# Cross-attention scores from high and low parts made ahead, and another order of the small steps around them

## The reference

```python
def _L0_xattn_ref(hidden_q, kv_c, ...):          # hidden_q = layernorm(x): 64 x 32 x 512, kv_c: 64 x 257 x 128
    q_hk = (hidden_q @ Wq.T).reshape(Bv, Sv, H, K)                 # 16 heads
    q_big = _apply_rope(jnp.einsum('bshk,hkq->bshq', q_hk, w_kc_q), sin_q, cos_q)
    kv_r = _apply_rope(kv_c, sin_k, cos_k)
    q_r = jnp.einsum('bshq,hqr->bhsr', q_big, W_qr)
    k_r = jnp.einsum('bld,hdr->bhlr', kv_r, W_kr)
    scores = jnp.einsum('bhsr,bhlr->bhsl', q_r, k_r)
    attn = jax.nn.softmax(scores, axis=-1)
    ctx_c = jnp.einsum('bhsl,bld->bhsd', attn, kv_r)
    ctx_lat = jnp.einsum('bhsd,hkd->bhsk', ctx_c, w_kc_kv)
    return ctx_lat.transpose(0, 2, 1, 3).reshape(Bv, Sv, H * K) @ Wo.T
```

## Time and profile before

| | us |
|---|---|
| median of 3 runs | 1603.32 (1601.59 to 1603.51) |
| the profiled execution | 1603.56 |
| its span, first to last instruction | 1601.4 |
| its mean granted TensorE clock | 0.972 of full speed |
| TensorE busy over the span | 1485.5 (93%) |
| VectorE busy | 1139.9 (71%) |
| ScalarE busy | 811.1 (51%) |
| GpSimd busy | 541.8 (34%) |

### The profile page before, as it was taken

One profiled execution on the slowest core, in us unless ns is written; L12 is line 12 of the kernel. 1 busy time (PEld: TensorE's weight loads), 2 busy tenths in 40 slices (PEclk: granted clock), 3 DMA queues, 4 the chain that ended last, 5 costly groups with the idle time before them and its releaser, 6 DMA issues. The chain is left out here.

```text
span 1601.4 us, 26509 instructions
## 1 busy us (share of the span) xinstructions
PE 1485.5 (93%) x8136; PEld 1123.1 (70%) x8136; DVE 1139.9 (71%) x1820; ACT 811.1 (51%) x1739; POOL 541.8 (34%) x594
## 2 busy tenths in 40 slices
PE   4799999999978999999999977999898899999997
PEld 3577777777746777777777766888443478787876
DVE  6888777887648788788788853777687735556466
ACT  4566565666545555555555543555211355554554
POOL 4244333442025554544545513221351202222021
PEclk9899999999989999999999988999898899999999
DMA  4223334243565444544544514000244100000000
GB/s 152 68 81 111 105 110 119 75 122 95 182 219 126 119 119 105 125 111 106 129 107 108 139 21 172 0 0 0 84 174 158 45 1 1 27 1 26 0 27 27
DMA packets 140917, 140.05 MB, mean 87 GB/s; under 512 B 84150, under 2 KB 111926, under 8 KB 139708
## 3 DMA queue, kind: packets, MB, share of 16 engines
q1 hardware_dynamic: 140284, 138.54, 30.0%
q10 hardware_dynamic: 576, 0.81, 0.2%
HBM read 109.88 MB, written 27.39 MB: 86 GB/s over the span
## 5 line engine op out<-in xcount | busy, mean ns | idle before, releaser
L997 ACT ACTIVATE c_e<-c_sc_ps,c_peak 128x257 f32<-128x257 f32 x256 | 119.6, 473 | 219.4 <-DVE c_peak L900 219.4
L878 POOL TENSOR_TENSOR c_mixed_low<-c_whole,c_mixed_high 128x512 fp32r<-128x512 f32 x64 | 81.9, 1279 | 211.0 <-ACT c_mixed_high L1017 211.0
L77 DVE TENSOR_TENSOR b_rot_parts_low<-b_rot,b_rot_parts_high 128x1536 fp32r<-128x1536 f32 x64 | 136.0, 2125 | 21.9 <-ACT b_rot_parts_high L541 21.9
L278 POOL TENSOR_TENSOR b_turned_raw<-b_turn_part 128x384 f32<-128x384 f32 x32 | 70.1, 2190 | 166.2 <-DVE b_key_parts_low L77 165.0
L1571 PE MATMUL f_ps<-f_right,f_left 128*128 128x512 f32 x256 | 115.7, 613 | 8.4 <-ACT f_raw L1614 6.1
L70 PE MATMUL c_out_ps<-c_shared_high,c_mixed_high 128*128 128x512 f32 x256 | 112.2, 438 | 11.1 <-issue 10.1
L324 DVE TENSOR_TENSOR b_rot<-b_w_qr,b_angle 128x1536 f32<-128x1536 f32 x64 | 119.2, 1862 | 0.2
L70 PE MATMUL b_ps<-c_shared_high,b_wq_parts_high 128*128 128x512 f32 x256 | 108.5, 424 | 6.5 <-DVE c_shared_low L77 6.5
L70 PE MATMUL e_mm_ps<-folded_high,e_h_t_high 128*128 128x512 f32 x256 | 106.4, 416 | 5.7 <-DVE e_h_t_low L77 5.6
L541 ACT ACTIVATE b_rot_parts_high<-b_rot 128x1536 fp32r<-128x1536 f32 x64 | 95.3, 1489 | 24.5 <-PE b_ps L72 17.0
L274 POOL TENSOR_TENSOR b_turn_part<-b_early,b_centre 128x384 f32<-128x384 f32 x64 | 82.1, 1303 | 72.2 <-DMA b_early<-early 70.5
(11 more groups left out here) (232 smaller groups left out, 3903.8 us busy)
## 6 DMA issues: line engine op xcount, KB each, us to landing
c_ends_spread<-end_weights SPq DMA_DIRECT2D x64, 256.0 KB, 4.3
carried_queries<-x SPq DMA_DIRECT2D x7, 2048.0 KB, 11.3
b_early<-early SPq DMA_DIRECT2D x15, 640.0 KB, 4.0
f_left<-ent_in SPq DMA_DIRECT2D x16, 512.0 KB, 5.4
f_right<-ent_out SPq DMA_DIRECT2D x16, 512.0 KB, 6.5
c_q_first<-carried_queries SPq DMA_DIRECT2D x32, 224.0 KB, 3.3
c_q<-carried_queries SPq DMA_DIRECT2D x32, 224.0 KB, 3.2
b_late<-late SPq DMA_DIRECT2D x16, 320.0 KB, 3.8
```

What stands on the lines that cost most here:

```text
L77: return nc.vector.tensor_tensor(low, value, high.bitcast(F32), ALU.subtract)
L878: nc.gpsimd.tensor_tensor(mixed[1][:, w, :, u], whole[:, u % 2].rearrange("p (h s) -> p h s", h=H), mixed[0][:, w, :, u].bitcast(F32), ALU ...
L997: last = nc.scalar.activation(e[:, v, c], sc_ps[:, 2 * v + c, 0:L], ACT.Exp, bias=peak[:, v, c:c + 1], accum_out=total[:, v, c:c + 1])
```

## The change

1. Scores: each 128x257 fp32 product becomes three fp32r products (`multiply_parts`) of high and low parts of the queries and of the keys, with the keys padded to 258 columns (a zero column). ScalarE makes the high parts (`round_queries`, `round_keys`) and GpSimd the low parts (`split_queries`, `split_keys`), two batches ahead.
2. `keep_ends` goes from GpSimd to VectorE, after `find_peak`.
3. The keys' turn goes from half 0 to half 1, its rounding too, and `split_kv` to the next batch's even step, after `find_peak`.
4. SyncE: the store of the ends is taken out of `spread_ends` and goes ahead of the batch's raw loads; the raw keys have two buffers instead of four; a batch's queries are loaded after the spread; before `holo.load` SyncE waits for the last rotation, because `part` now lies in `spare`.
5. The last two heads of the first two batches' queries are no longer copied by ScalarE but loaded from `staged` (`staged_queries`), after the last output weights.
6. The angles of the next part are made in three pieces instead of two; `keep_moments` goes to j = 6 and `square_row` to j = 4.

Cut to its core:

```diff
             crossing.output_weights(sp, w_vo_dram, 2)
+            sp.wait_ge(qc_stored, 8 * HPAIRS)
+            crossing.staged_queries(sp, staged)
...
-                    if isinstance(U, int) and U >= 2 * HPAIRS - 2:
-                        at = (H - 2 + ab) * S + base
-                        nc.scalar.activation(crossing.q[:, :, at:at + G], ps[:, QC_BANK + ab].rearrange("p (b s) -> p b s", b=B)[:, 0:2], ACT.Copy)
...
+    def staged_queries(self, sp, staged):
+        for u in range(2):
+            sp.dma_start(self.q[:, u, (H - 2) * S:].bitcast(F32), staged[:, u].rearrange("p h s -> p (h s)")).then_inc(self.q_loaded[u], 16)
...
-        part = sb("c_part", [P, 2, L])
+        part = spare[:, 0:2 * L].rearrange("p (n l) -> p n l", n=2)
+        q_high = sb("c_q_high", [P, 2, H * S], F32R)
+        keys = pair("c_key", [P, 2, LE])
...
+            def store_ends(i, u):
+                b, v = BT * i + u, u % 2
+                sp.wait_ge(ended, 2 * b + 2)
+                sp.dma_start(ends_dram[bass.ds(b, 1)].rearrange("b p c -> p (b c)"), ends[:, v]).then_inc(ends_stored[v], 16)
+
             def spread_ends(i, u):
...
-                wait(sp, mix_taken, b - 1)
-                sp.wait_ge(ended, 2 * b + 2)
-                sp.dma_start(ends_dram[at].rearrange("b p c -> p (b c)"), ends[:, v]).then_inc(ends_stored[v], 16)
                 sp.wait_ge(ends_stored[v], 32 * i + 16 * (u // 2) + 16)
...
-                    if known(i, 1):
-                        wait(sp, rotated_, b - BT + 1)
-                        crossing.load(sp, b, u)
                     if isinstance(b, int) and b < 2:
                         continue
-                    wait(sp, scored, 2 * (b - BT) + 2)
-                    sp.dma_start(q[u][:, 0:(H - 2) * S], ...
-                    sp.dma_start(q[u][:, (H - 2) * S:], ...
+                    if known(i, 1):
+                        store_ends(i - 1, u)
+                    wait(sp, rotated_, b - 1)
+                    crossing.load(sp, b, u % 2)
                     if known(i, 1):
                         spread_ends(i - 1, u)
+                    wait(sp, scored, 2 * (b - BT) + 2)
+                    sp.dma_start(q[u][:, 0:(H - 2) * S].bitcast(F32), ...
+                    sp.dma_start(q[u][:, (H - 2) * S:].bitcast(F32), ...
...
             in_tiles(sp, tile)
+            sp.wait_ge(rotated_, B)
             holo.load(sp, holo_loaded)
             for u in range(BT):
+                store_ends(TILES - 1, u)
                 spread_ends(TILES - 1, u)
...
             def rotate(b, u, tile_of_b):
-                pool.wait_ge(raw_loaded[u], 48 * (tile_of_b + 1))
+                pool.wait_ge(raw_loaded[u % 2], 48 * (2 * tile_of_b + u // 2 + 1))
...
-            def keep_ends(n, i, u, half):
-                pool.wait_ge(normed, n + 1)
...
+            def split_queries(b, u):
+                pool.wait_ge(q_rounded, b + 1)
+                nc.gpsimd.tensor_tensor(q[u], q[u].bitcast(F32), q_high[:, u % 2].bitcast(F32), ALU.subtract).then_inc(q_split, 1)
+
+            def split_keys(b, u):
+                pool.wait_ge(key_rounded, b + 1)
+                nc.gpsimd.tensor_tensor(keys[1][:, u % 2], kv_even[u], keys[0][:, u % 2].bitcast(F32), ALU.subtract).then_inc(key_split, 1)
...
-                    keep_ends(n, i, u, half)
+                    if half == 0 and not (isinstance(b, int) and (b == 0 or b + 1 >= B)):
+                        split_keys(b + 1, (u + 1) % BT)
                     if half == 0 and not (isinstance(b, int) and b + 2 >= B):
                         rotate(b + 2, (u + 2) % BT, i + (u + 2) // BT)
+                    if half == 1 and not (isinstance(b, int) and b + 2 >= B):
+                        split_queries(b + 2, (u + 2) % BT)
                     if half == 1 and (u or known(i, 1)):
                         split_mixed(b - 1, (u - 1) % BT, w if u else 1 - w)
...
+            def keep_ends(n, i, u, half):
+                v = u % 2
+                if half == 0:
+                    wait(dve, ends_stored[v], 32 * i + 16 * (u // 2))
+                nc.vector.tensor_tensor(ends[:, v, 2 * half:2 * half + 2], e[:, half, :, END], inverse[:, half], ALU.mult).then_inc(ended, 1)
...
                         find_peak(n + 1, 1 - half)
+                    keep_ends(n, i, u, half)
+                    if half == 0 and (u or known(i, 1)):
+                        split_kv(b - 1, (u - 1) % BT)
                     if half == 1 and (u or known(i, 1)):
                         add_end(i - (u == 0), (u - 1) % BT)
                     if more:
                         normalise(n + 1, 1 - half)
                     split_turned(n, u, half)
-                    if half == 0:
-                        split_kv(b, u)
...
-            dve.wait_ge(scored, 2 * B)
+            dve.wait_ge(rotated_, B)
...
+            def round_queries(b, u, t):
+                act.wait_ge(q_loaded[u], queries_in(u, t))
+                wait(act, scored, 2 * b - 2)
+                nc.scalar.activation(q_high[:, u % 2], q[u].bitcast(F32), ACT.Copy).then_inc(q_rounded, 1)
+
+            def round_keys(b, u):
+                act.wait_ge(rotated_, b + 1)
+                wait(act, scored, 2 * b - 2)
+                nc.scalar.activation(keys[0][:, u % 2], kv_even[u], ACT.Copy).then_inc(key_rounded, 1)
...
                     round_turned(n, b, u, half)
-                    if half == 0:
+                    if half == 1:
                         round_kv(b, u)
                     if half == 1 and (u or known(i, 1)):
                         round_mixed(b - 1, (u - 1) % BT, i if u else i - 1, w if u else 1 - w)
+                    if not (isinstance(b, int) and b + 2 >= B):
+                        if half == 0:
+                            round_queries(b + 2, (u + 2) % BT, i + (u + 2) // BT)
+                        else:
+                            round_keys(b + 2, (u + 2) % BT)
...
+            round_keys(0, 0)
+            round_queries(0, 0, 0)
             exponential(0, 0)
+            round_keys(1, 1)
+            round_queries(1, 1, 0)
...
                 if half == 0:
-                    pe.wait_ge(q_loaded[u], queries_in(u, t))
-                    pe.wait_ge(rotated_, b + 1)
+                    pe.wait_ge(q_split, b + 1)
+                    pe.wait_ge(key_split, b + 1)
...
-                    last = nc.tensor.matmul(sc_ps[:, 2 * half + c, 0:L], q[u][:, at], kv_t[u], start=True, stop=True)
+                    last = multiply_parts(nc, sc_ps[:, 2 * half + c, 0:LE], [q_high[:, u % 2, at], q[u][:, at]], [a[:, u % 2] for a in keys], True, True)
...
-                    if half == 0:
+                    if half == 1:
                         turn_kv(b, u)
```

More of the change, by code:

```diff
@@ L691, in __init__ @@
         raw, swapped = sb("c_raw", [P, 2, L]), sb("c_swapped", [P, 2, L])
+        self.raw_pair, self.swapped_pair = raw[:], swapped[:]
         self.raw, self.swapped = ([a[:, u] for u in range(2)] for a in (raw, swapped))
-        self.q = sb("c_q_first", [P, 2, H * S])
-        self.keys = sb("c_keys_first", [P, L])
+        self.q = ctx.enter_context(nc.sbuf_tensor("c_q_first", [P, 2, H * S], F32R))
+        self.keys = sb("c_keys_first", [P, L + 1])
         self.q_loaded = [sem(f"c_q_loaded{u}") for u in range(BT)]
-        self.pool_chained, self.rotated = sem("c_pool_chained"), sem("c_rotated")
+        self.pool_chained, self.rotated, self.padded = sem("c_pool_chained"), sem("c_rotated"), sem("c_padded")
         self.table_loaded = sem("c_table_loaded")
-        self.raw_loaded = [sem(f"c_raw_loaded{u}") for u in range(BT)]
+        self.raw_loaded = [sem(f"c_raw_loaded{u}") for u in range(2)]
         self.staged_out = sem("b_staged_out")
@@ L730, in rotate_first @@
         nc.gpsimd.tensor_tensor(part[:, 1], self.swapped[0], self.table[:, 1], ALU.mult).then_inc(self.pool_chained, 1)
+        nc.gpsimd.memset(self.keys[:, L:], 0.0).then_inc(self.padded, 1)
         pool.wait_ge(self.pool_chained, 2)
-        nc.gpsimd.tensor_tensor(self.keys[:], part[:, 0], part[:, 1], ALU.add).then_inc(self.rotated, 1)
+        pool.wait_ge(self.padded, 1)
+        nc.gpsimd.tensor_tensor(self.keys[:, 0:L], part[:, 0], part[:, 1], ALU.add).then_inc(self.rotated, 1)
     def first(self, sp):
@@ L844, in tile @@
                              x_tiles[bass.ds(i, 1)].rearrange("t p d -> p (t d)")).then_inc(x_loaded, 16)
-            for u in range(2, BT):
-                crossing.load(sp, u, u)
             in_tiles(sp, tile)
+            sp.wait_ge(rotated_, B)
             holo.load(sp, holo_loaded)
             for u in range(BT):
+                store_ends(TILES - 1, u)
                 spread_ends(TILES - 1, u)
@@ L858, in rotate @@
             def rotate(b, u, tile_of_b):
-                pool.wait_ge(raw_loaded[u], 48 * (tile_of_b + 1))
-                nc.gpsimd.tensor_tensor(part[:, 0], raw[u], table[:, 0], ALU.mult).then_inc(pool_chained, 1)
```

(17 more changed lines are left out.)

43 lines of the change are left out of this document (23 added, 20 removed).

## The result

The changed kernel takes 1643.0 us (1641.74 to 1644.35), the kernel before, run beside it, 1602.94: a ratio of 1.0251, 95% interval 1.0234 to 1.0269. The forecast was 1638. The profiled execution took 1642.47, its span is 1640.7, 39.3 more than before, and its mean clock 0.966.

The account below looks back on a forecast made before the run. The prediction took two crossing loops between TensorE and VectorE, 7.27 and 7.15 us a batch, as the bound. 1603.56 + 5.5 (start) + 11 (end) + 17.5 (port) = 1637.6, so 1638 us, range 1608 to 1664.

Parts of the forecast that it names:

- The products: Score steps: six fp32r products of 258 columns, 0.12 each, 0.72 a step instead of 0.87, a gain of 0.15.
- the weight load that the sentence on the Trainium skill put at the edge: Score products: a weight load of 107 ns, about as long as 258 columns stream, could put the step between its bounds.
- The regular batch: Cross-attention batch without a row sum: 7.24 us against 7.27 before, so nearly nothing gained.
- loop B: VectorE's even step, then TensorE's odd turn, three heads and score: 7.15 before, 7.24 with the key turn, becoming the bound.
- the batch of the row sum: Batch where a tile's row sum is added: the odd peak slips 0.5, making 7.6.
- the port never met: Rival: keep ahead of the subtraction or too small to block, -4 in the tiles, 1616 in all; chance 0.27.
- TensorE's saving: About 0.3 us a batch saved on TensorE, of which nearly nothing arrives in the period.
- The port: VectorE's odd keep waits for GpSimd's 1.27 subtraction of queries in two batches a tile: +1.25 a tile, +17.5 in all.
- GpSimd and ScalarE have room: Added work per batch fits: GpSimd 2.0 at most on 3.7 of 7.39 busy, ScalarE 0.68+0.41 on 4.0.
- SyncE's later store is covered: Store of the ends goes some 1.7 later; keep to next add_end 6.8 to 7.0, covered by 0.3.
- The start: First queries' last two heads come by a later DMA: first score 466.5 against 460.78, +5.5, bounds 4 and 7.
- The end: Last tile: store and spread wait behind holo.load and the last rotation, stalling VectorE 11, bounds 8 and 13.

Follow-up runs that it names:

- e11: Changed kernel with GpSimd's subtraction of the queries cut from 512 to 16 columns, keep as changed: 1618.7 us, ratio 1.0094.
- e12: Changed kernel with keep and odd steps' normalisation by per-partition factors, and two orders in SyncE's queue changed: 1606.4 us, ratio 1.0011.
- e10: Kernel before with the keep on VectorE and the odd steps' normalisation as two multiplications by per-partition factors: 1597.5 us, ratio 0.9965.
- e5: Kernel before with the keep alone moved to VectorE, after the peak: 1602.1 us, ratio 0.9983.
- e2: Changed kernel with the keep on VectorE as two one-column multiplications by a per-partition factor: 1618.2 us, ratio 1.0095.
- e3: Changed kernel with the rotation's products in their own buffer and no SyncE wait before the phases' loads: 1643.3 us, ratio 1.0239.
- e4: Changed kernel with staged queries ahead of the last output weights and phases' loads after the last tile's third-batch spread: 1634.5 us, ratio 1.0184.
- e6: Kernel before with its normalisation as two multiplications by per-partition factors: 1601.4 us, ratio 0.9991.
- e9: Changed kernel with the keep by per-partition factors and two orders in SyncE's queue changed, normalisation as changed: 1605.8 us, ratio 1.0014.
- e7: Changed kernel with keep and normalisation both as multiplications by per-partition factors: 1631.7 us, ratio 1.0175.

## Why the prediction was right, and where it was not

- *The products*: 0.72 a step forecast, 0.73 measured, 0.12 a product; the weight load that the sentence on the Trainium skill put at the edge does not show in it.
- *The regular batch*: loop B at 7.24, the batch of the row sum at 7.6, a tile of 29.3 with the port never met. e11, which is that case, has 7.23, 7.65 and 29.35; unblocked batches of the changed kernel are 7.23 too. TensorE's saving went where the forecast put it, into the loop through VectorE's even step: a shorter odd step gains nothing in e12, and 0.23 a tile in the kernel before (e10 against e5).
- *The port*: the mechanism, the step it meets and the odd keep as the place were right; e2, e11 and e5 show it from three sides. Which keeps are met was taken the wrong way round. I had the keep of a regular batch 0.05 ahead of the subtraction, and the keep behind a row sum inside it. The regular keep does come 7.85 after the odd peak before it (647.39 against 639.54), but the subtraction 7.70 (647.24) and not 7.9, so it is met; the keep behind the row sum (640.15) comes after the subtraction has ended and takes 0.15. So it is in 13 tiles out of 13: the first odd keep behind the row sum 0.15, the second 1.0 to 1.2. Measured tiles alternate between 7.23, 7.86, 7.23, 8.86 and 7.23, 7.86, 7.91, 8.34, the row sum in the last batch: against the free tile (7.23, 7.65) a blocked regular batch costs 0.63 to 0.68 and the row-sum batch 0.7 to 1.2. Two or three batches of a tile are blocked, where I had two. Its price was mis-sized by this: 30.8 a tile forecast, 31.26 measured, 1.9 instead of 1.5 over the free tile. That it came so near with the order reversed is luck. Against the kernel before I also took too short a tile: 29.55, a mean with a shorter early tile in it, where 13 regular ones have 29.78, which is 0.23 of the error the other way.
- *GpSimd and ScalarE have room, SyncE's later store is covered*: right. Of 48 add_ends from 524 to 905 in the changed kernel one waited, 0.08.
- *The start*: first score at 466.5 forecast, 466.34 measured; first peak +5.5 and +5.16. Counted from ScalarE's last copy of the query path it is 6.3 later (7.50, and 460.78-459.57 = 1.21 before); that path itself ended 0.73 earlier, which the sum did not have.
- *The end*: 11, bounds 8 to 13; it was 12.5, of which 9.27 are the wait and 3.05 the slow TensorE behind it, which had been put into the upper bound only. The spread went out 7.1 after the rotation (951.57), not 8.6, and landed 3.8 later, not 4.3. That the wait for the rotation is its cause is half of the truth: without it 4.45 of 9.27 stay (e3), and the order of the loads has to change as well (e4).
- *The first two tiles*: 0 forecast, 5.9 measured, the one term that was missing. Of it 1.7 is the port again, in the fourth, seventh and eighth batch (7.53, 7.77 and 7.95 us, where before has 7.05, 7.25 and 7.29), with odd keeps of 0.99, 1.10 and 0.71. Some 4.2 is in the second and the fifth batch (8.63 and 9.25, before 6.69 and 6.94), over which the granted clock is 0.71 and 0.82; the fifth has a keep of 1.17 as well. e11 has odd keeps of 0.15 there and still takes 60.53. (e2 has 55.89, but in the shortest of its five executions.) The shorter products are not shown to be the cause: e5, with the scores of before, has a batch of 8.84 at a clock of 0.56 (467.27 to 476.11), e6 one of 8.27 at 0.79 (475.50 to 483.80). In the first tile TensorE has no heads to project. The windows view of a stretch of 16 us behind it, in e11, in the changed kernel and before:

```profile
496.00:512.00 16.00, 11.74 (x52) 10.01 (x51) 12.85 (x24) 9.28 (x28) 8.02 (x10) 0.71 0.48 108
```

```profile
496.00:512.00 16.00, 9.84 (x56) 8.26 (x55) 13.23 (x25) 9.36 (x29) 10.65 (x13) 0.89 0.56 115
```

```profile
491.00:507.00 16.00, 11.21 (x58) 8.61 (x57) 13.51 (x24) 9.55 (x30) 7.87 (x13) 1.00 0.49 117
```

The granted clock is 0.71, 0.89 and 1.00. TensorE is not busier in one than in another by much (11.7, 9.8 and 11.2 us, and a slow product counts as busy longer), and e9 kept 1.00 in that stretch with the same products. What decides it there stays open.
- *The rest of the program*: 4.2 less than before in this execution, which happens to offset most of the missing term.

So 34 us were forecast and 39.3 measured in the span: the three costs and their mechanisms were right, the port met other keeps than I had and cost 0.4 a tile more, and the early tiles and the rest of the program, +5.9 and -4.2, were not in the sum; that these two nearly cancel is luck too.

## What to carry to other kernels

Before a small step is moved from GpSimd to VectorE, look at what GpSimd will run when its turn comes: here a VectorE step with two SBUF tensors, of 0.15 us by itself, waited for the end of a GpSimd step of 1.28, and everything behind it in VectorE's order waited too. A step of one column by a per-partition factor did not wait, a step of 256 columns did, so the remedy for the small step is no remedy for the wide one. A margin of 0.05 us in a forecast of when two engines meet decides nothing: the steps it was added up from were off by 0.2. A change that is slower as a whole can hold a part that is worth keeping: the moved keep alone, in the kernel before, cost nothing, and with a shorter odd normalisation it gave 0.35%.

## What the runs showed of the hardware

- A multiplication of four numbers a partition took 0.15 us with GpSimd idle (640.15 in the changed kernel) and up to 1.25 behind a GpSimd subtraction of 128x512 (1.28). Two one-column steps by a factor took 0.33 in the midst of such a subtraction.
- Two 128x256 steps by a factor took 0.62 with GpSimd idle and 1.29 with two GpSimd products running one after the other (e7); one 128x512 step of two tensors took 0.69 and, in e2 under the same products, 0.82 on average.
- Six fp32r products of 258 columns took 0.73 at full clock, 0.12 each, and 0.22 each at the start (466.71 to 467.58 in the changed kernel), where the granted clock was 0.50 over 460 to 468, the lower of its two levels.
